# Banded attention as one stream of 32 tiles with its gated network inside, and a re-laid expert stage

## What is computed

```python
def _layer(x, wqkv, qs, ksc, wo, lg, lb, w1, b1, w2, b2):
    h = shift_token(x)                       # half of the features from the token before
    q, k, v = jnp.split(h @ wqkv, 3, axis=-1)   # 8 heads of 64
    q = l2norm(q) * qs
    k = l2norm(k) * ksc
    q, k = rotary_xpos(q, k)
    o = local_attention(q, k, v)             # each token sees itself and the 64 before
    x = x + o @ wo
    h = layernorm(shift_token(x)) * lg + lb
    a, g = jnp.split(h @ w1 + b1, 2, axis=-1)   # 341 each
    x = x + (a * jax.nn.gelu(g, approximate=False)) @ w2 + b2
    return x
```

```python
logits = jnp.einsum('bntd,des->bntes', grouped, Wc) + bc + tie
perm = (logits == jnp.max(logits, axis=-3, keepdims=True))
permuted = jnp.einsum('bntd,bntes->bnesd', grouped, perm)
inner = relu(jnp.einsum('bnesd,esdf->bnesf', permuted, W1) + b1)
res = jnp.einsum('bnesf,esdf->bnesd', inner, W2) + b2
out = jnp.einsum('bnesd,bntes->bntd', res, perm)
```

## Time and profile before

| | us |
|---|---|
| median of 3 runs | 2715.95 (2713.83 to 2716.72) |
| the profiled execution, its own time | 2716.01 |
| its span, first to last instruction | 2714.2 |
| first banded stage, first matmul to last sum | 377.8 to 794.3 |
| second banded stage, first to last sum | 837.0 to 1251.6 |
| first expert stage | 2302.0 to 2398.6 |
| second expert stage | 2607.9 to 2705.6 |
| TensorE busy | 2225.2, 82% of the span |
| VectorE busy | 1772.0, 65% |
| ScalarE busy | 1385.8, 51% |
| GpSimd busy | 718.8, 26% |
| mean granted TensorE clock | 0.894 |

### The profile page before, as it was taken

One profiled execution on the slowest core, in us unless ns is written; L12 is line 12 of the kernel. 1 busy time (PEld: TensorE's weight loads), 2 busy tenths in 40 slices (PEclk: granted clock), 3 DMA queues, 4 the chain that ended last, 5 costly groups with the idle time before them and its releaser, 6 DMA issues. The chain is left out here.

```text
span 2714.2 us, 42839 instructions
## 1 busy us (share of the span) xinstructions
PE 2225.2 (82%) x15196; PEld 1524.2 (56%) x15196; DVE 1772.0 (65%) x4423; ACT 1385.8 (51%) x3630; POOL 718.8 (26%) x472
## 2 busy tenths in 40 slices
PE   6999979889887987978447887768776988689978
PEld 4888846636643653653347774433424765556648
DVE  6777748759746965964656663356456997637863
ACT  3555537738734764864411226563636764326750
POOL 0000016516502642630033420000012976051000
PEclk9999999989988989999678898888987999778986
DMA  1000021100002101001012320000001221100010
GB/s 56 14 19 15 7 72 22 23 20 21 21 5 75 25 17 24 21 16 48 0 36 58 74 46 0 12 12 6 4 12 56 86 70 60 45 10 2 2 65 17
DMA packets 79043, 80.92 MB, mean 30 GB/s; under 512 B 28624, under 2 KB 63952, under 8 KB 77808
## 3 DMA queue, kind: packets, MB, share of 16 engines
q1 hardware_dynamic: 78832, 78.19, 10.1%
HBM read 53.94 MB, written 8.52 MB: 23 GB/s over the span
## 5 line engine op out<-in xcount | busy, mean ns | idle before, releaser
L1014 ACT ACTIVATE window_s<-window_s,window_soft 128x128 f32<-128x128 f32 x512 | 197.7, 394 | 5.0 <-DVE window_soft L1177 5.0
L1084 POOL TENSOR_TENSOR window_s<-window_s,window_soft 128x512 f32<-128x512 f32 x128 | 133.2, 1041 | 218.5 <-DVE window_soft L1114 218.4
L1092 POOL TENSOR_TENSOR window_pa<-window_pa,window_pb 128x1024 f32<-128x1024 f32 x64 | 151.5, 2368 | 148.8 <-DVE window_pb L1159 148.8
L1177 DVE CUSTOM_DVE_ANT_0 window_s<-ps,window_mask,window_nrn 128x128 f32<-128x128 f32 x512 | 148.7, 346 | 46.7 <-PE ps L859 29.9
L3127 DVE TENSOR_TENSOR_SCAN mamba_bx<-ps,mamba_ab 128x256 f32<-128x256 f32 x256 | 154.5, 667 | 18.9 <-PE ps L2913 18.9
L822 PE MATMUL ps<-window_wa,window_sh 128*128 128x512 f32 x256 | 131.3, 638 | 41.4 <-DVE window_pb L1159 28.4
L3297 ACT ACTIVATE rope_p<-ps,rope_mx 128x128 f32<-128x128 f32 (+1 forms) x256 | 104.3, 419 | 53.1 <-DVE rope_mx L3351 53.1
L2910 PE MATMUL ps<-mamba_m,mamba_xt 128*128 128x129 f32 x512 | 102.9, 283 | 29.6 <-ACT mamba_m L2985 20.6
L83 PE MATMUL ps<-x,consts 128*128 128x512 f32 x120 | 77.0, 801 | 46.1 <-PEq L53 40.5
L3015 POOL TENSOR_TENSOR h<-mamba_bx,mamba_cbr 128x1024 f32<-128x1024 f32 x32 | 89.3, 2796 | 93.2 <-DVE mamba_bx L3127 92.7
L2910 PEld LDWEIGHTS ps<-mamba_m,mamba_xt 128*128 128x128 f32 x512 | 82.3, 197 | 49.1 <-issue 49.1
(11 more groups left out here) (607 smaller groups left out, 6235.9 us busy)
## 6 DMA issues: line engine op xcount, KB each, us to landing
mamba_cbr<-mamba_c SPq DMA_DIRECT2D x32, 512.0 KB, 3.7
window_vs<-window_vt SPq DMA_DIRECT2D x64, 128.0 KB, 2.3
delta_xi<-delta_x SPq DMA_DIRECT2D x16, 512.0 KB, 5.1
switch_w<-in_switch_w SPq DMA_DIRECT2D x4, 2048.0 KB, 10.1
window_wa<-in_window_wa SPq DMA_DIRECT2D x4, 1152.0 KB, 6.8
linattn_wb<-in_linattn_wb SPq DMA_DIRECT2D x6, 513.0 KB, 3.5
window_wb<-in_window_wb SPq DMA_DIRECT2D x4, 537.5 KB, 7.7
window_sh<-y SPq DMA_DIRECT2D x16, 128.0 KB, 2.2
```

What stands on the lines that cost most here:

```text
L1014: a = nc.scalar.activation(s[:, k % 2, e, c, :], s[:, k % 2, e, c, :], ACT.Exp, scale=-1.0, bias=soft[:, k % 2, e, 1, c:c + 1], accum_out= ...
L1084: nc.gpsimd.tensor_tensor(s[:, k % 2, e], s[:, k % 2, e], soft[:, k % 2, e, 3, :].unsqueeze(2).to_broadcast([P, QC, P]), ALU.mult)\
L1092: nc.gpsimd.tensor_tensor(own, own, pb[:, :, :, :].rearrange("p a h d -> p (a h d)"), ALU.add)\
L1177: v = nc.vector.tensor_tensor_reduce(s[:, k % 2, e, c, :], K.ps[:, B_S + e, toks(c, P)], mask[:, k % 2, :], nrn[:, k % 4, h:h + 1], 3e38, ...
```

## The change

**Banded stage.** The 2 x 16 tiles become one stream of N = 32 steps with one common prologue and ten steps behind it (SLOTS = 42). The norm and gated network of block b are spread over steps FIRST + 4b to FIRST + 4b + 5, that is 8 to 13 for the first block: a small piece in two places of each step, `early(i)` and `late(i)`. They use only banks 2 (B_V) and 5 (B_S), one piece at a time, so `project_v` and `scores` now wait until the piece before them has been read (`early_moved`, `mean_moved`, `late_moved`). In a step TensorE's order becomes `turn_qk`, `project_out`, `early`, `scores`, `project_qk`, `mean`, `turn_p`, `project_v`, `late`, `values`. ScalarE moves the first two gate parts out of PSUM with a bias, and does all three Gelus in the fourth step of the block, with a table load ahead of them and one behind. The first shifts start at the first block of the outer norm instead of the fourth; the shifts for the second layer are issued inside the stream.

**Expert stage.** The bias goes into VectorE's first operation of the choice. `z` is laid out as group by slot, so a copy writes 128 neighbouring elements and the first expert matmul reads its moving columns 128 elements apart; each engine copies from a bank of its own without waiting for the other. `b2` enters by TensorE as 16 matmuls; the sums are made with 32 columns of weights (`perm`) and 128 moving columns, tokens on the partitions, then copied and transposed back. Transposes, sums and turns back of the four blocks are staggered, and ScalarE shares the copies.

```diff
+    N, BLOCKS = DEPTH * TILES, DEPTH * NJ
+    SLOTS = N + 10
+    FIRST = 2 * TPW
+    def part(i):
+        b, r = divmod(i - FIRST, TPW)
+        return (b if 0 <= b < BLOCKS else None), (b - 1 if 1 <= b <= BLOCKS else None), r
...
+            def early(i):
+                b, last, r = part(i)
+                pe.wait_ge(st.v_copied, up_to(i))
...
+                if r == 0 and last is not None:
+                    hidden(last, 1)
+                if r == 1 and b is not None:
+                    var(b)
+                if r == 2 and b is not None:
+                    gate(b, 0)
+                if r == 3 and b is not None:
+                    gate(b, 2)
+
+            def late(i):
...
+                if r == 0 and last is not None:
+                    hidden(last, 2)
+                if r == 1 and last is not None:
+                    mlp_out(last)
+                if r == 2 and b is not None:
+                    gate(b, 1)
+                if r == 3 and b is not None:
+                    hidden(b, 0)
...
-                    if 2 <= i < TILES + 2:
-                        turn_qk(base + i - 2)
-                    if i < TILES:
-                        project_qk(base + i)
-                    if 2 <= i < TILES + 2:
-                        scores(base + i - 2)
-                    if i >= 4:
-                        project_out(base + i - 4)
...
+            for i in stream:
+                b, last, r = part(i)
+                if 2 <= i < N + 2:
+                    turn_qk(i - 2)
+                if 4 <= i < N + 4:
+                    project_out(i - 4)
+                if i >= FIRST:
+                    early(i)
+                if 2 <= i < N + 2:
+                    scores(i - 2)
+                if i < N:
+                    project_qk(i)
+                if r == 0 and b is not None:
+                    early_moved(i)
+                    mean(b)
+                if 3 <= i < N + 3:
+                    turn_p(i - 3)
+                if i < N:
+                    project_v(i)
+                if i >= FIRST:
+                    late(i)
+                if 3 <= i < N + 3:
+                    values(i - 3)
...
+            def gelus(b):
...
+                nc.scalar.activation(gl[0:m, 2, :], K.ps[0:m, B_V, :], ACT.Gelu, bias=b1g(b // NJ, 2))\
+                    .then_inc(st.g_moved, 1)
+                act.wait_ge(st.g_moved, 3 * b + 2)
+                nc.scalar.activation(gl[:, 0:2, :], gl[:, 0:2, :], ACT.Gelu).then_inc(st.gelu_done, 1)
+                nc.scalar.preload_act_table_set("natural_log_exp_and_others")
...
+                if i < N:
+                    square(i)
+                if r == 1 and b is not None:
+                    rstd(b)
+                if r == 2 and b is not None:
+                    move_gate(b, 0)
+                if r == 3 and b is not None:
+                    gelus(b)
+                if 3 <= i < N + 3:
+                    move_p(i - 3)
+                if 2 <= i < N + 2:
+                    exps(i - 2, 0)
...
-    z = st.sb("z", [P, ES, NG])
+    z = st.sb("z", [P, NG, ES])
...
-                                          z[:, 4 * q + r, :], start=True, stop=True)
+                                          z[:, :, 4 * q + r], start=True, stop=True)
...
-                    mm = nc.tensor.matmul(K.ps[:, 4 + j, toks(g % 16, GT)], resm[:, g, :], perm[:, toks(g, GT)],
-                                          start=True, stop=True)
...
+                for t in range(TPW):
+                    for g in range(4):
+                        n = 4 * (TPW * j + t) + g
+                        mm = nc.tensor.matmul(K.ps[32 * g:32 * g + 32, 4 + j % 2, toks(t, P)], perm[:, toks(n, GT)],
+                                              resm[:, n, :], start=False, stop=True, skip_group_check=True)
```

More of the change, by code:

```diff
@@ L908, in mean, with var @@
                     .then_inc(st.mean_ready, 1)
-            def var(l, j):
-                pe.wait_ge(st.square_ready, NJ * l + j + 1)
-                nc.tensor.matmul(K.ps[:, j, :], K.mean_mat, sq2[:, toks(j)], start=True, stop=True)\
+            def var(b):
+                pe.wait_ge(st.square_ready, b + 1)
+                nc.tensor.matmul(K.ps[:, B_V, :], K.mean_mat, sq2[:, toks(b % NJ)], start=True, stop=True)\
                     .then_inc(st.var_ready, 1)
[L915 to L930, removed]
@@ L932, in mlp_out, with gate @@
-            def mlp_out(l, j):
-                k = NJ * l + j
-                if j == 1:
-                    pe.wait_ge(st.log_ready, NJ * (l + 1))
-                if j >= 2:
-                    pe.wait_ge(st.y_ready, NJ * (l + 1) + j - 1)
+            def gate(b, c):
+                l, j = divmod(b, NJ)
+                m = HC[c][1]
+                pe.wait_ge(st.norm_ready, b + 1)
+                if b == 0 and c == 0:
+                    pe.wait_ge(st.wb_ready, 16 * DEPTH)
+                nc.tensor.matmul(K.ps[0:m, (B_V, B_S, B_V)[c], :], w1g(l, c), hn[:, toks(j)], start=True, stop=True)\
+                    .then_inc(st.hid_g, 1)
@@ new lines, in _ @@
+            for i in stream:
+                b, last, r = part(i)
+                if 4 <= i < N + 4:
+                    move_o(i - 4)
+                if 3 <= i < N + 3:
+                    recip(i - 3, 0)
+                if 1 <= i < N + 1:
+                    move_v(i - 1)
+                    norms(i - 1)
+                if 3 <= i < N + 3:
+                    recip(i - 3, 1)
+                if 2 <= i < N + 2:
+                    negate(i - 2)
+                    mask_and_max(i - 2, 0)
+                if r == 0 and last is not None:
+                    gated(last, 1)
+                if 4 <= i < N + 4:
+                    attended(i - 4)
+                if i < N:
+                    cosines(i)
+                if r == 0 and b is not None:
+                    centre(b)
+                if 2 <= i < N + 2:
+                    mask_and_max(i - 2, 1)
+                if i < N:
+                    sines(i)
+                if r == 0 and last is not None:
+                    gated(last, 2)
+                if r == 1 and b is not None:
+                    normalise(b)
+                if r == 1 and last is not None:
+                    finish(last)
+                if r == 3 and b is not None:
+                    gated(b, 0)
@@ new lines, in pick @@
+            def pick(j, u):
+                pe.wait_ge(st.chosen_copied, j + 1)
+                if u:
+                    pe.wait_ge(st.picked_act, seen[j, 0])
+                    pe.wait_ge(st.picked_dve, seen[j, 0])
+                for t in range(TPW):
+                    for e in range(2):
+                        g = 2 * u + e
+                        rows, tile = slice(32 * g, 32 * g + 32), toks(TPW * j + t, P)
+                        mm = nc.tensor.matmul(K.ps[:, j + 4 * e, toks(t, P)], h_tm[rows, tile], perm_tm[rows, tile],
+                                              start=True, stop=True)
+                mm.then_inc(st.picked, 1)
@@ new lines, in _ @@
+            for n in range(0, ES // 8, 2):
+                act.wait_ge(st.h2_ready, n + 1)
+                if n:
+                    act.wait_ge(st.h2_copied, n)
+                nc.scalar.activation(result_to(n), K.ps[:, (4 + n) % 8, :].rearrange("p (q g) -> p q g", g=NG), ACT.Copy)\
+                    .then_inc(st.h2_copied, 1)
+            moved(0)
+            moved(2)
+            for j in range(NJ):
+                if j + 1 < NJ:
+                    moved(4 * j + 4)
+                    moved(4 * j + 6)
+                result(j)
```

554 lines of the change are left out of this document (276 added, 278 removed).

## The result

| | before | after |
|---|---|---|
| median, runs side by side | 2714.89 (2712.82 to 2716.72) | 2689.14 (2684.52 to 2692.27) |
| ratio, 95% interval | | 0.9904 [0.9887, 0.9921] |
| span of the profiled execution | 2714.2 | 2686.4 |
| mean granted TensorE clock | 0.894 | 0.917 |
| first / second banded stage | 416.5 / 414.6 | 424.9 / 425.0 |

The account below looks back on a forecast made before the run. The prediction saw TensorE, VectorE and ScalarE all nearly full in a banded step, with slack only between layers. Banded stages 0, expert stages 45 us: 2716.0 - 0.5 - 45 = 2670.5, range 2620 to 2712.

Parts of the forecast that it names:

- Ordinary step: Banded stream step without network: ScalarE's loop sums to 9.33 us, VectorE's to 9.29, against 8.07 before.
- Network steps: Banded stream, four steps per network block: 11.4, 12.0, 10.4 and 13.5 us, a block 47.3.
- Table load: ScalarE in a block's fourth step: each load costs its recorded 1.28 us, without the skill's extra drain.
- The head: Banded stage's start: first shift 2.8 us earlier, scores another 2.0 earlier; then a fill step 8.4, ordinary steps 9.33.
- The tail: Banded stage's end after step 32: a step of 10.4 us, drain and remaining network 38, falling clock 4.
- Expert stage, the front: Choice and copies before the first expert matmul: it comes 15 us earlier, taken as 14.5.
- Expert stage, the read with a step: First expert round reading `z` 128 elements apart: between nothing and 5.9 us extra, taken as 1.5.
- Expert stage, the end: New sums and turns back: 26 us instead of 35.5, a gain of 9.5.
- Full overlap: Rival: banded stream runs at TensorE's own sum, 10.2 us instead of 11.8 in network steps; 2574, half 2622; chance 0.13.
- the double table load: Rival: each load in the banded stream costs a further load's length, 20.5 us per stage; 2711.5; chance 0.05.
- The falling clock: Rival: TensorE's clock falls in the stream; ten of 64 steps at half clock eat the gain, sixteen give 2748; chance 0.13.
- The third: Rival: expert stages' last sums stay at half clock and the spread read doubles its round; 2698; chance 0.07.

Follow-up runs that it names:

- e7: The kernel before with only TensorE's order in a step changed to output projection, scores, then projection of queries and keys: 2782.52 against 2717.15, ratio 1.0241.
- e5: The changed kernel with Square in place of the Gelus and without the table loads around them: 2650.55, ratio 0.9758.
- e3: The changed kernel with TensorE's old order in a step, projection of queries and keys before scores, then output projection: 2612.28 against 2716.55, ratio 0.9621.
- e1: The kernel before with only the expert stages of the changed kernel: 2668.54 against 2716.55, ratio 0.9823.
- e9: The kernel of e8 with the network's weights loaded behind the first shifts and waited for in step 8: 2603.91 against 2715.64, ratio 0.9584.
- e6: The changed kernel with `z` laid out slot by group again, so the expert matmul reads neighbouring columns: 2677.94, ratio 0.9855.
- e8: The changed kernel with both the old TensorE order and `z` slot by group: 2605.99, ratio 0.9597; run beside e9, 2608.16, ratio 0.9605.

## Why the prediction was right, and where its size was off

The sign and the range held; the gain was 26 us instead of 45. Two figures of the forecast have no source: the 0.5 us taken off in the sum, where the banded stages are put at 0, and a `z` that is full at 2326.5, where its terms give 2326.8. Neither matters to the result. Step by step:

- **Ordinary step, 9.33.** Measured 9.41 to 9.48, with the loop's terms as they were summed. e7 shows it without the stream. Right.
- **Network steps.** From scores to scores block 0 took 46.9 us instead of 46.0, four blocks 48.3 or 48.4 instead of 47.3, and the sixth 49.0 instead of 48. The mis-sized term is in the first step, 11.96 instead of 11.4: `project_v`, `hidden` and `values` behind `centre`, put at 2.6 us, took 3.2 (612.50 to 615.73). The second and third steps are 0.24 over each, the fourth as forecast. I had followed the loops of ScalarE and VectorE; TensorE's own queue was not followed as a loop. In the second step its row is nearly unbroken: 11.33 us of instructions and one wait of 0.91 before `project_v`, with the 2.67 us of `mlp_out` behind it. From step 8 to step 32 that is 289.4 us against 283.2: +6.2 a stage.
- **Table load, 1.28.** Right, by e5 (1.24 by the medians, 1.2 in a step, 1.27 in a block). The Trainium skill, "ScalarE: Activation LUTs", section What ACT_TABLE_LOAD costs, has about 2.66 a switch; the runs decide against it here.
- **The head.** First scores 24.6 us after the stage's start by forecast; 27.35 measured in the first stage (404.59 less 377.24), 26.19 in the second: +2.75 and +1.6. The term that failed is the 2.8 us of an earlier shift, and it failed in two ways. In the first stage the shift wasn't issued earlier at all (10.49 us after the start, 387.73 less 377.24, against 10.28 before), since the norm's first eight matmuls ran at half clock, 6.72 us instead of 3.67. No edit goes with that: e3 has 3.67 there, and e1, whose banded stages are those of before, 5.37. In the second stage it was issued as forecast, but I took its DMA to be as quick as before, and it stood behind the weights (e9). In the first stage the two steps after it took 9.41 and 11.05 instead of 8.4 and 9.33, +2.7: the first of them was a fill step and still had the new order's length, and the second has some records at half clock (scores 1.94, projection 2.79). With 0.5 in the next four, +5.9 in all; the second stage comes to the same (10.21 and 11.36 for the two).
- **The tail.** 50.0 us from step 32's scores to the last sum, 52.4 forecast: -2.4. The sum of the three, 9.7, is the distance between the 424.9 of the trace and the forecast's 415.2.
- **Where the stream's gain went.** The drain of 73 us between the layers is gone, as meant, and the order ate it: 4.4 us in each block of steps and 1.4 in each ordinary one (e3). That is the cost the prediction named; its alternative, 10.2 a step, was priced as a rival of *this* kernel, but it is closer to what the old order gives (43.9 for four, 11.0 a step).
- **Expert stage, the front.** The first expert matmul came 29.4 us after the stage's start instead of 39.6: -10.2, and -14.7 in the second stage; forecast -14.5. In the first stage the transposes before it fell to half clock (0.60 and then 1.11 for four), in the second they didn't (0.66).
- **Expert stage, the read with a step.** +4.7 instead of +1.5; the forecast's upper bound was 5.9. This was the wrong end of the range. The Trainium skill, "SBUF — State Buffer", section Door 1, had pointed to it; the trace agrees in direction (10.6 us of busy time against 5.4 in e6).
- **Expert stage, the end.** 21.6 us instead of 35.5: -13.9, forecast -9.5. The sums took 4.3 us (four times 1.08) instead of 7.7, and of the 2.5 us that I had added for a mix of clocks little was needed: the clock was 0.78 for the first 6.8 us and 1.00 from there on. The misses of front, read and end cancel, and 44.6 against 45 is right by luck as well as by working.
- **The rivals.** Full overlap and the double table load are refuted by the ordinary step and e5. The falling clock is refuted in its size: it fell in some fourth steps and cost about 0.3 us each; TensorE was busy 86.5% in the stream, where the forecast had 80. The third (half clock in the sums with a doubled read) was half right: the read did nearly double, the sums ran at 1.00.

## What to carry to other kernels

When a step is a loop over several engines, look at what an independent instruction covers where it stands: the projection filled the time in which ScalarE copied the keys, and behind the scores the same instruction, 1.9 us long, lay on the path and cost about 1.4 us a step, 65 to 77 us in all. Judge the parts of a large change one by one: here the stream was worth 56 us (e3 against e1) and the order inside it cost 77 (e3 against the whole). Follow every engine's own queue as a loop, the busiest first, and count what is already in the DMA queues ahead of a transfer that is issued earlier.

## What the runs showed of the hardware

- 256 small matmuls whose 64 moving columns lie 128 elements apart took 10.6 us, with neighbouring columns 5.4 in e6 (0.041 and 0.021 each) and 5.86 in the kernel before. The read with a step took 10.59 at a granted clock of 0.80 and 10.24 at 1.00 in after, 10.59 at 0.80 and 10.88 at 1.00 in e3, so the clock isn't what bounds it.
- A copy of 128x512 out of PSUM took VectorE 0.69 us with a plain write. With a step of 64 elements it took 1.01 in the kernel before, where ScalarE and VectorE copy by turns, and 1.02 to 1.33 in e6 (1.25 on average in the first stage), where both copy at once. Whether the other engine's copy is what lengthens it wasn't tested.
- The sums turned round, 32 columns of weights and 128 moving, took 1.08 us for 32 instructions at full clock, where the kernel before took 0.19 us for each of 128 with the sides exchanged, at half clock.
- A shift of 128 KB that was issued behind all of the stage's weights and tables (two loads of 1152 KB, two of 537.5, one of 256 in the DMA view) had its reader start 5.3 and 5.5 us after its issue; without the two of 537.5 ahead of it, 3.1 and 3.0 (e8 and e9, run side by side, first and second banded stage).
